# Turning the quantized inner values of an FP4 network on VectorE and through HBM, with their down-projection one chunk later

## The reference

```python
def fp4_linear(x, w):
    xq = fp4_quant_dequant(x)
    wq = fp4_quant_dequant(w)
    return jnp.einsum('bsk,nk->bsn', xq, wq)
gate = fp4_linear(x, w_gate)      # 256 -> 704
y = fp4_linear(x, w_up)
h = jax.nn.silu(gate) * y
return fp4_linear(h, w_down)      # h is quantized again, 704 -> 256
# the whole: x + s * silu(ffn(xn)), s from the attention and the plain network
```

## Time and profile before

| | us |
|---|---|
| median of 3 runs | 1111.18 (1109.03 to 1113.21) |
| the profiled execution, its time | 1108.42 |
| the profiled execution, its span | 1106.7 |
| matrix engine, matmuls busy | 1083.8 (98%) |
| matrix engine, weight loads busy | 985.9 (89%) |
| VectorE busy | 906.8 (82%) |
| ScalarE busy | 511.8 (46%) |
| GpSimd busy | 52.2 (5%) |

### The profile page before, as it was taken

How to read it: one execution, slowest core, us unless ns; L and a number is a source line. 1 busy time by engine, 2 the same in 40 slices (tenths; PEclk the granted TensorE clock), 3 DMA queues, 4 the chain that set the end, 5 groups by cost and what they waited for, 6 DMA issues and landing times.

```text
span 1106.7 us, 18820 instructions
## 1 busy us (share of the span) xinstructions
PE 1083.8 (98%) x7016; PEld 985.9 (89%) x7016; DVE 906.8 (82%) x1978; ACT 511.8 (46%) x1422; POOL 52.2 (5%) x71
## 2 busy tenths in 40 slices
PE   9999999999999999999998799999999999999997
PEld 6998999999989989999987699999999999999897
DVE  6888888898888988998677878878878778787786
ACT  6654646546546465465554533233323333233332
POOL 0000000000000000000000102020010202020200
PEclk9999999999999999999999999999999999999999
DMA  7455355454553554535447402011110203030010
GB/s 236 147 167 166 112 186 162 143 183 130 179 163 126 168 162 158 183 116 166 145 146 205 110 20 71 25 39 58 39 58 20 77 2 96 1 95 1 17 42 20
DMA packets 113466, 120.01 MB, mean 108 GB/s; under 512 B 8672, under 2 KB 108384, under 8 KB 113376
## 3 DMA queue, kind: packets, MB, share of 16 engines
q1 hardware_dynamic: 113376, 118.82, 34.0%
HBM read 65.75 MB, written 53.04 MB: 107 GB/s over the span
## 4 chain that ended last, share of the span: by engine, by line
PE 79%; DVE 12%; DMA 5%; ACT 2%; issue 1%; SPq 1%; POOL 0%; DVEq 0%; POOLq 0%
PE ps L248 59%; PE ps L638 4%; PE ps L679 4%; PE ps L673 4%; PE ps L659 3%; DMA moved<-work 3%; DMA r_gate<-moved 2%; PE ps L759 2%; PE ps L590 1%; DVE work L1429 1%; DVE r_k L1377 1%; DVE r_v L1433 1%; SPq L385 1%; DVE r_v L1446 1%; DVE work L1402 1%
## 5 line engine op out<-in xcount | busy, mean ns | idle before, releaser
L248 PE MATMUL ps<-r_k,r_gate_up 128*128 128x512 f32 x768 | 187.6, 394 | 4.0 <-DVE work L1429 3.3
L248 PEld LDWEIGHTS ps<-r_k,r_gate_up 128*128 128x128 f32 x768 | 141.0, 188 | 32.1 <-DVE work L1429 3.7
L248 PE MATMUL ps<-r_o,onT 128*128 128x256 f32 x768 | 107.0, 288 | 0.1
L898 ACT ACTIVATE work<-ps 128x128 f32<-128x128 f32 x256 | 67.4, 278 | 81.4 <-PE ps L679 81.4
L248 PEld LDWEIGHTS ps<-r_q,r_v 128*128 128x128 f32 x768 | 99.5, 191 | 5.9 <-issue 2.1
L248 PE MATMUL ps<-hT,r_k 128*128 128x512 f32 x378 | 103.2, 408 | 0.0
L248 PE MATMUL ps<-r_q,r_v 128*128 128x256 f32 x768 | 102.7, 283 | 0.0
L1035 ACT ACTIVATE r_v<-work 128x512 fp32r<-128x512 f32 x64 | 40.5, 633 | 131.9 <-DVE work L1429 131.9
L248 PE MATMUL ps<-hT,r_q 128*128 128x512 f32 x384 | 98.2, 391 | 0.0
L248 PE MATMUL ps<-r_v,hT 128*128 128x512 f32 x384 | 97.4, 390 | 0.0
L248 PEld LDWEIGHTS ps<-r_o,onT 128*128 128x128 f32 x768 | 95.7, 190 | 0.3 <-DVE onT L1157 0.3
(11 more groups left out here) (147 smaller groups left out, 2047.4 us busy)
## 6 DMA issues: line engine op xcount, KB each, us to landing
moved<-work SPq DMA_DIRECT2D x63, 512.0 KB, 2.9
r_gate<-moved SPq DMA_DIRECT2D x252, 128.0 KB, 2.6
work<-in_L_attn_hidden_states SPq DMA_DIRECT2D x16, 512.0 KB, 5.4
kept<-work SPq DMA_DIRECT2D x9, 514.0 KB, 4.4
kept_h<-work SPq DMA_DIRECT2D x9, 512.0 KB, 3.7
work<-kept SPq DMA_DIRECT2D x8, 514.0 KB, 6.1
kept_xq<-work SPq DMA_DIRECT2D x8, 512.0 KB, 5.8
work<-kept_xq SPq DMA_DIRECT2D x32, 128.0 KB, 2.8
```

The source lines that it names most:

```text
L248: done = pe.matmul(out_ap, a, b, start=first and n == 0, stop=last and n == 2, skip_group_check=skip)
L898: done = act.activation(squares[:, c, :], ps[:, B_O, c * P:(c + 1) * P], ACT.Square, accum_out=small[:, OS, c:c + 1])
```

## The change

The 31 sets other than the last are no longer turned by the matrix engine. `quantize_done` now turns them by two VectorE instructions in blocks of 32x32: one of 640 columns and one of the last 64 columns taken twice (128 columns), in place of the copy of 64. SyncE's new `exchange4` stores the tile to HBM (384 KB), waits for the landing, and loads it back in four pieces that put the blocks where they belong; a piece is on 32 partitions. ScalarE writes the high part of the turned set by one instruction of 768 columns from SBUF (`hq`), which now stands after the silu of slice 2c+1. VectorE's `hq_lo` is one instruction of 768 columns from SBUF, and stands after `quantize_constants`. `down4` of set m-1 stands at the end of chunk m for every chunk, so that set 3's goes from just after `gate_up4` of the next block's chunk 0 to that chunk's end (`LAG4 = 1`). The order of SyncE's other transfers is fitted around the exchanges. The last set is still turned by the matrix engine.

Wdown's high half is written by ScalarE in two instructions, and its low half by VectorE in two instructions of 1024 columns (before block 0, and in its chunk 1), where GpSimd did it by one of 2048.

```diff
+                def exchange4(m):
+                    through = kept_h4[m % 2]
+                    sp.wait_ge(h4_quantized, m + 1)
+                    sp.dma_start(through.rearrange("a p x -> p a x"), h4_turned_sb).then_inc(hq_stored, 16)
+                    sp.wait_ge(hq_stored, 16 * (m + 1))
+                    if m:
+                        sp.wait_ge(hqT_ready, m)
+                    for q in range(QUADS):
+                        sp.dma_start(hq_in[q * QUAD:(q + 1) * QUAD],
+                                     through[q].rearrange("(b p) x -> p b x", b=QUADS)).then_inc(hq_loaded, 16)
...
-                pool.wait_ge(wdown_hi, 1)
-                pool.tensor_tensor(wdown[:, LO, :, :], raw_wdown, wdown[:, HI, :, :].bitcast(F32),
-                                   ALU.subtract).then_inc(wdown_ready, 1)
...
                         gate_up(n, 2 * c)
                         if c:
                             down(n, 2 * c - 1)
-                            turn4(n, c - 1)
                         gate_up(n, 2 * c + 1)
                         down(n, 2 * c)
-                        if c:
-                            down4(n, c - 1)
+                        if n * CH + c >= LAG4:
+                            down4(n * CH + c - LAG4)
                     down(n, FT - 1)
-                    turn4(n, CH - 1)
                     if not final:
                         gate_up4(n + 1, 0)
-                        down4(n, CH - 1)
...
+                def hq(m):
+                    act.wait_ge(hq_loaded, 16 * QUADS * (m + 1))
+                    if m:
+                        act.wait_ge(out4_done, m)
+                    act.activation(hqT[:, HI, :, :].rearrange("p f (a t) -> p f a t", t=QUAD), turned4_sb(hq_in), ACT.Copy)\
+                       .then_inc(hq_hi, 1)
...
+                        silu_gate(n, 2 * c + 1)
+                        if LAG4 == 1 and earlier >= 0:
+                            hq(earlier)
+                        hmT_hi(n, 2 * c + 1)
+                        if earlier >= 0:
+                            gate_out(earlier)
...
-                def quantize_done(c, mine):
+                def quantize_done(c, m, mine):
                     data, again = h4[:, c % 2, 0:N4], h4[:, c % 2, N4:N4P]
                     settled2(dve.tensor_tensor(groups_of(data), groups_of(data), wide(scale4[:, 1, :]), ALU.mult), mine)
-                    dve.tensor_copy(again, data[:, N4 - REST4:N4]).then_inc(h4_quantized, 1)
+                    if m:
+                        dve.wait_ge(hq_stored, 16 * m)
+                    split = FULL4 * P
+                    to = turned4_sb(h4_turned_sb)
+                    dve.transpose(to[:, 0:FULL4], data[:, 0:split].rearrange("p (f a t) -> p f a t", a=QUADS, t=QUAD))
+                    rest = data[:, split:N4].rearrange("p (d a t) -> p d a t", d=1, t=QUAD)
+                    dve.transpose(to[:, FULL4].rearrange("p (d a) t -> p d a t", d=2),
+                                  rest.to_broadcast([P, 2, QUADS // 2, QUAD])).then_inc(h4_quantized, 1)
...
+                def hq_lo(m):
+                    dve.wait_ge(hq_hi, m + 1)
+                    dve.tensor_tensor(hqT[:, LO, :, :].rearrange("p f (a t) -> p f a t", t=QUAD), turned4_sb(hq_in),
+                                      hqT[:, HI, :, :].rearrange("p f (a t) -> p f a t", t=QUAD).bitcast(F32),
+                                      ALU.subtract).then_inc(hqT_ready, 1)
...
+                def wdown_lo(i):
+                    dve.wait_ge(wdown_hi, i + 1)
+                    part = slice(i * FT // 2, (i + 1) * FT // 2)
+                    dve.tensor_tensor(wdown[:, LO, part, :], raw_wdown[:, part, :], wdown[:, HI, part, :].bitcast(F32),
+                                      ALU.subtract).then_inc(wdown_ready, 1)
+                wdown_lo(0)
...
                         mlp_lo(n, 2 * c)
-                        if c:
-                            hq_lo(n, c - 1)
                         if c == CH - 1 and not final:
                             xT_lo_of(n + 1, range(KD))
                         quantize_constants(data, mine)
+                        if LAG4 == 1 and n * CH + c >= LAG4:
+                            hq_lo(n * CH + c - LAG4)
                         mlp_product(n, 2 * c + 1)
```

More of the change, by code:

```diff
@@ L161, in build @@
         x2 = one.cut(CH, ROW)
+        x2_end = one.at
         state = one.cut(CH - 1, P)
@@ L229, in build @@
         x2b = two.cut(CH, ROW)
+        two.at = max(two.at, x2_end)
+        h4_turned_sb = two.cut(QUADS, T4 * QUAD)
+        hq_in = work[:, down4_at:down4_at + QUADS * T4 * QUAD].rearrange("p (a x) -> p a x", a=QUADS)
         two.at = 0
@@ L483, in _ @@
                 sp.wait_ge(x2_stored, 16 * (BLOCKS + 1))
[L484 to L490, removed]
+                def exchange4(m):
[8 more added lines that the diff above has]
+                                     through[q].rearrange("(b p) x -> p b x", b=QUADS)).then_inc(hq_loaded, 16)
+                for n in range(BLOCKS):
+                    exchange4(n * CH)
+                    if n == 0:
+                        sp.wait_ge(h2_turned, BLOCKS + 1)
+                        sp.dma_start(kept_h2[BLOCKS - 1].rearrange("a p x -> p a x"),
+                                     leaving.rearrange("p a i x -> p a (i x)")).then_inc(h2_stored, 16)
+                        sp.wait_ge(wdown_ready, 2)
+                        load_xb(0)
+                    if n:
+                        sp.wait_ge(res_ready, n)
+                        sp.dma_start(out_blocks[n - 1], res).then_inc(out_stored, 16)
+                        load_xb(n)
+                    exchange4(n * CH + 1)
+                    exchange4(n * CH + 2)
                     if n + 2 < BLOCKS:
@@ L493, in _ @@
                         load_turned(xq_in, kept_xq[n + 2], xq_loaded)
+                    if n < BLOCKS - 1:
+                        exchange4(n * CH + 3)
+                    if n + 2 < BLOCKS:
                         sp.wait_ge(xT_ready, (n + 1) * TURNS + TURNS)
@@ L726, in down @@
                         pe.wait_ge(wdown_ready, 1)
+                    if n == 0 and f == FT // 2:
+                        pe.wait_ge(wdown_ready, 2)
                     pe.wait_ge(hmT_ready, n * FT + f + 1)
@@ L829, in networks @@
                             down(n, 2 * c - 1)
-                            turn4(n, c - 1)
                         gate_up(n, 2 * c + 1)
                         down(n, 2 * c)
-                        if c:
-                            down4(n, c - 1)
+                        if n * CH + c >= LAG4:
+                            down4(n * CH + c - LAG4)
                     down(n, FT - 1)
-                    turn4(n, CH - 1)
                     if not final:
                         gate_up4(n + 1, 0)
-                        down4(n, CH - 1)
                     else:
-                        last_down4(n, CH - 1)
+                        for m in range(LAST4 + 1 - LAG4, LAST4):
+                            down4(m)
+                        last_turn4()
+                        last_down4()
                 for n in range(BLOCKS - 1):
@@ L1065, in _ @@
                 act.wait_ge(wdown_loaded, 16)
-                act.activation(wdown[:, HI, :, :], raw_wdown, ACT.Copy).then_inc(wdown_hi, 1)
+                for f in range(0, FT, FT // 2):
+                    act.activation(wdown[:, HI, f:f + FT // 2, :], raw_wdown[:, f:f + FT // 2, :], ACT.Copy)\
+                       .then_inc(wdown_hi, 1)
                 normed_h2(BLOCKS + 1, xq_new)
@@ L1512, in networks @@
                     if final:
-                        hq_lo(n, CH - 1)
+                        for m in range(LAST4 + 1 - LAG4, LAST4):
+                            hq_lo(m)
+                        last_hq_lo()
                     dve.wait_ge(mlp_done, n + 1)
```

78 lines of the change are left out of this document (46 added, 32 removed).

## The result

The changed kernel takes 1119.43 us (median of 5 runs, 1119.13 to 1123.03), the kernel before 1110.07 (5 runs, 1107.74 to 1113.21). The ratio is 1.0103, 95% interval 1.0085 to 1.0122: slower by 11.4 us, between 9.4 and 13.5 (the two medians lie 9.4 apart). The forecast was slower by 17 us, at 1127.

A forecast was written before the change was run, and what follows sets the result against it. The prediction took VectorE's in-order chain, with its new waits, to bound the kernel: links of 62.7 us a block against 60.28, so 7 x 2.4 = +17 us, giving 1127 us, range 1099 to 1145.

The forecast's parts named there:

- VectorE's chain takes the lead, and what the matrix engine saves turns into waits: Waits of about 5 us a block at `down4`, second up product, chunk 0's `gate_up`; block 62.7 against 60.28; chance 0.62.
- The first rival: Matrix engine stays the bound and VectorE's waits are absorbed: 1088 us, or 1091 from the median; chance 0.14.
- The links: Start-to-start times between first `product4`s: chunks 13.5, 16.9, 14.65, 15.25 us, block's end 2.4; sum 62.7 a block.
- chunk 2's 8.9 us to the end of `hq`: From chunk 2's first `product4` to the high part's end behind the silu: 8.9 us; VectorE, ready at 8.2, waits 0.7.
- VectorE idles 2 us before `product4` of chunk 1: In chunk 0, `product4` stands before `quantize_subtract`, so VectorE idles 2 us where it idled 0.65.
- The exchange, 6.9 us: Through HBM, from the transposes' end to landing: 6.9 us, ends 6.3 and 9.0; adds a 1.5 us wait in chunk 1.
- The estimate by the Trainium skill: The exchange from 2.0 us fixed per transfer, plus bytes and issues: 6.4 us, 0.5 less a block; not used in the sum.
- Block 0, net 0, give or take 1: Wdown's stall goes, net 1.3 us gained; the links behind it lose 1.7; together 0, give or take 1.
- Block 7 loses as much as the others in its first three chunks: Last block: same loss in three chunks, nothing more to turn on VectorE in its last chunk, tail as it was.
- The sum: Whole kernel: 7 x 2.4 = +17 us, on 1108.4 profiled, 1125.4; 1128.2 from the median; given as 1127.
- If that engine kept its lead: Matrix engine rid of 31 x 0.65 = 20.2 us would need 57.7 us a block, and that would be the gain.

The follow-up runs named there:

- e12: Second run, for its profile, of the changed kernel with chunk 0's `product4` moved behind the turning: 1106.1 us, period 60.35.
- e2: Changed kernel with LAG4 = 2, a set's down-projection two chunks behind its turning: 1109.72 us, ratio 1.0007 to the kernel before.
- e9: Changed kernel with LAG4 = 2, `product4` behind the turning, and the first `quantize_constants` instruction before `mlp_lo` of slice 2c: 1098.79 us, ratio 0.9903 to the kernel before.
- e6: Changed kernel without VectorE's two transposes in blocks 1 to 7: 1107.38 us, ratio 0.9976 to the kernel before.
- e5: Kernel before without the matrix engine's transposes in blocks 1 to 7, nothing added: 1097.23 us, ratio 0.9902.
- e1: Changed kernel with one move, chunk 0's `product4` behind the turning: 1107.57 us, ratio 1.0005 to the kernel before.
- e8: Changed kernel with LAG4 = 2, `product4` behind the turning, and x's four low parts on GpSimd: 1117.57 us, ratio 1.0073 to the kernel before.
- e3: Changed kernel with both LAG4 = 2 and `product4` behind the turning: 1108.92 us, ratio 0.9994 to the kernel before.

## Why the prediction was right, and where its sizes were off

1. *VectorE's chain takes the lead, and what the matrix engine saves turns into waits* ("about 5 us a block"): right. Measured 4.9 more, at the three places named; at `gate_up` it waits in chunk 1 (0.77) more than in chunk 0 (0.40), which alone was named. e12, e2 and e9 show that VectorE's order sets the period, and e6 that its added work is part of it. The first rival, 1088, did not hold: the engine at 98% lost 18.9 us of weight loads (985.9 - 967.0) and the kernel got slower. The rule of the Trainium skill that pointed to it (Perfetto Trace Analysis, Identifying the Most-Contended Engine), to optimize the engine of highest occupancy first, fits this case by half: in e5 that engine was relieved of 2.6 us a block with nothing added elsewhere, and 1.35 came out.
2. *The links.* Chunk 0 13.5, measured 876.71 - 863.13 = 13.58; chunk 1 16.9, measured 16.63; chunk 2 14.65, measured 14.49; chunk 3 and the end 17.65, measured 17.41. Together 62.7 against 62.1 in block 4 and 62.26 in the mean. The terms of chunk 2's 8.9 us to the end of `hq` add up to 8.8, which would make its wait 0.6, as measured (0.62). The new instructions came as taken: transposes 0.85 and 0.27 (0.80 and 0.30), `hq_lo` 0.96 busy, 0.87 to its successor (0.89).
3. *VectorE idles 2 us before `product4` of chunk 1*: 2.38. I had its cost only as a late start of the next link. What the prediction did not say is that moving this one call gives the whole loss back (e1); e2 gives as much and leaves the call where it is, so the loss needs both, the late turning and a down-projection only one chunk behind.
4. *The exchange, 6.9 us*: mis-sized. From the transposes' end at 880.55 to ScalarE's start at 886.71 it is 6.16: loads issued 2.63 after the store and not 2.99, landed 2.2 after the last issue and not 2.6. The estimate by the Trainium skill (DMA: Bandwidth & Descriptors, the two cost components), 6.4, was the nearer one. Of the 0.74 gained 0.5 was lost again, as GpSimd's additions stood beside VectorE (875.95 to 880.07) and stretched two instructions by 0.08 and 0.42; I had counted up to 0.3 there and taken 0. The wait before `hq_lo` is 0.83 in place of 1.5.
5. *Block 0, net 0, give or take 1*: right. From the stage's start to block 1's first `product4` it is 675.91 - 612.01 = 63.90 after and 678.95 - 615.75 = 63.20 before: +0.7. And that is no more than the clock took: the matrix engine's clock was low at the stage's start in this execution, 0.50 granted (the lower of its two levels) from 612 to 614 and 0.69 from 614 to 616. Before the stage's start it had waited 2.95 us, as in every one of these kernels; behind the same wait the kernel before and e2 had 1.00. The first of these weight loads after, and in e2:

```profile
612.01 1.68 PEld L257 LDWEIGHTS ps<-r_gate,r_k 128*128 128x128 f32 x6 [2.95 <-ACT work L1061]
```

```profile
611.95 0.94 PEld L257 LDWEIGHTS ps<-r_gate,r_k 128*128 128x128 f32 x6 [2.97 <-ACT work L1061]
```

The first `mlp_product` comes 8.00 us after the stage's start in place of 9.87 before, and 7.21 after it in e2, whose list is the same up to there. So the low clock cost 0.8, and the stall's end is worth 2.7 without it, where the prediction had 3.7 - 1.2 = 2.5. Behind it, from chunk 1's first `product4` to block 1's, 2.6 were lost (50.05 against 47.47), for 1.2 of Wdown and 1.7 of links.
6. *Block 7 loses as much as the others in its first three chunks*, 2.4: they lost 2.2 (0.79 + 1.75 - 0.34), and what follows gave 0.4 back, so that the block and its tail lost 1.8.
7. *The sum*: 0.7 + 11.9 + 1.8 = 14.4 in place of 17. The term that was too large is the loss of a block, 2.4 for 1.98, 0.27 of it in chunk 1 with its shorter exchange, 0.16 in chunk 2 and 0.24 from chunk 3 on, less 0.08 in chunk 0. In this one execution the attention also gave 3.7 back. The time of 5 runs, +11.4, lies under the stage's 14.4, the upper end of its interval at 13.5; 0.8 of the 14.4 is the low clock of point 5. That the attention is really shorter in the changed kernel isn't shown: its end lies between 611.7 and 616.9 in nine profiles of kernels made from the changed one (mean 614.1) and between 613.6 and 615.8 in four made from the one before (mean 614.9).
8. *"If that engine kept its lead": 57.7 us a block* was no floor that the kernel could reach by this change. e5 puts it at 58.93 with the turning free, since VectorE already set the block's end. This did not enter the forecast, but it overstated the first rival by 1.2 x 7 = 9 us.

## What to carry to other kernels

Before work is moved off the busiest engine, write down the other engine's list in start-to-start times and look for where it is already the one waited for: shares of 98% and 82% hid that both set parts of the block. In a list that an engine takes in order, an instruction that waits goes behind all work that is ready; here the place of one call was worth 12 us, as much as the change cost. The last step is the idle gap that every chunk has: with one instruction of 0.5 us put into it the kernel was 10 us faster here, about 7 of them by the gap itself, and 1.5 to 2.5 in the kernel before. A gap is worth filling only where its engine leads, here in two chunks of four. And look at a block chunk by chunk before a sum is explained: 0.37 us of gap times four would have matched the 1.40 gained, and two of the four gave nothing.

## What the runs showed of the hardware

- Elementwise instructions of GpSimd and VectorE on SBUF slow each other. In e8 four of 128x512 took 7.37 us on GpSimd, 1.84 each, and VectorE's beside them 1.78 for 0.69 and 1.97 and 1.88 for 0.89. A GpSimd multiplication of 128x256 took 0.71 where VectorE read PSUM or idled, and 1.42 beside VectorE's scaling in e9, which kept its 0.89; in e3 it took 1.04 and the scaling 1.31. VectorE's transposes at 922.60 in e8 stand beside the last of the four (until 923.71) and were not slowed (0.84).
- The granted clock can fall to its lower level behind a wait of the matrix engine of 2 to 3 us, and need not. At the stage's start, behind the same 2.95 us, it was 1.00 in the kernel before and 0.50 for 2 us in the changed one, which cost 0.8 us. In e8 it fell in every other block, behind the same 2.14 us, and those blocks took 1.07 us more.
- One of ten executions of e1's kernel took 2716.4 us, the other nine 1107.52 in the median; one of the kernel before, measured beside it, took 2771.9. In the profile of the first (span 2714.7) the matrix engine is 100% busy and a product of 512 columns takes 0.83 us in place of 0.40. Its page has no row of the granted clock, and the 1.000 recorded for it does not fit products of twice the time. The cause is open.
- The end of the attention, which these edits leave alone, lay up to 5 us apart from one profile to another, as much as some of the edits are worth. A period between equal instructions is the steadier measure: 60.28 and 60.27 in two kernels whose blocks are the same.
